# Summing eight products: GpSimd's halving and two VectorE adds replaced by one VectorE tensor_reduce

## What is computed

```
x = x + layernorm(attention(layernorm(x)))
x = x + layernorm(ffn(layernorm(x)))

# attention: 512-wide rows are cut in tokens of C = 16 channels, two branches of 8 channels;
# a window has 8 tokens (a row piece in one branch, a column piece in the other)
attn = softmax(q * 8**-0.5 @ k.T)          # 8 x 8 for each window
out  = attn @ v + depthwise_conv(v)
att  = concat(branch0, branch1) @ proj_w + proj_b
tok  = tok + layernorm(att) * ln_w + ln_b
```

## Time and profile before

| | us |
|---|---|
| runs of the kernel before (3) | 1411.92, 1413.1, 1414.27 |
| median | 1413.1 |
| span of the profiled execution | 1412.0 |
| VectorE busy in it | 1243.1 |
| TensorE busy in it | 1044.9 |
| GpSimd busy in it | 765.3 |
| ScalarE busy in it | 523.5 |

### The profile page before, as it was taken

The page is one execution under the profiler, slowest core; times in us unless marked ns, Lnnn a source line. Parts: engine busy times, 40 slices in busy tenths (PEclk is TensorE's granted clock), DMA queues, the critical chain, the costliest instruction groups (busy, mean ns, idle before and its releaser), DMA issues. The chain is left out here.

```text
span 1412.0 us, 14344 instructions
## 1 busy us (share of the span) xinstructions
PE 1044.9 (74%) x4483; PEld 531.0 (38%) x4483; DVE 1243.1 (88%) x1716; ACT 523.5 (37%) x790; POOL 765.3 (54%) x492
## 2 busy tenths in 40 slices
PE   5524368777887688868787778876887688678896
PEld 3312244343443343434343334433444244233442
DVE  4999999999899999999899998999899999975313
ACT  2235335332452434414253324524344143523332
POOL 2555336565576555765456644765557664754322
PEclk9756669889898899979898899988899799889998
DMA  4100200103001210102101030012101020012000
GB/s 128 30 0 13 77 6 24 30 1 89 1 16 45 60 31 1 38 21 59 30 3 57 0 89 1 15 45 59 30 1 46 15 60 1 7 53 60 7 24 30
DMA packets 70266, 46.07 MB, mean 33 GB/s; under 512 B 39616, under 2 KB 64192, under 8 KB 70208
## 3 DMA queue, kind: packets, MB, share of 16 engines
q1 hardware_dynamic: 65344, 45.10, 11.5%
q10 hardware_dynamic: 4864, 0.32, 0.2%
HBM read 28.63 MB, written 16.78 MB: 32 GB/s over the span
## 5 line engine op out<-in xcount | busy, mean ns | idle before, releaser
L599 PE MATMUL ps_up<-xhi,wu 128*128 128x512 f16 x512 | 218.8, 427 | 145.1 <-DVE fuse L1190 144.9
L864 POOL TENSOR_TENSOR sum<-prod 128x1024 f32<-128x1024 f32 x64 | 154.4, 2412 | 171.1 <-DVE prod L1031 171.1
L873 POOL TENSOR_TENSOR sum<-prod 128x1024 f32<-128x1024 f32 x64 | 158.6, 2478 | 156.4 <-DVE prod L1031 156.4
L1031 DVE TENSOR_TENSOR prod<-probs,qkvl 128x512 f32<-128x512 f32 x256 | 240.0, 1000 | 0.0
L1031 DVE TENSOR_TENSOR prod<-qkvl 128x512 f32<-128x512 f32 x256 | 222.2, 927 | 6.3 <-ACT qkvl L713 6.3
L599 PE MATMUL ps_up<-xlo,wu 128*128 128x512 f16 x512 | 218.2, 426 | 0.0
L599 PE MATMUL ps_gate<-xhi,wg 128*128 128x512 f16 x512 | 207.5, 405 | 3.6 <-DVE xlo L1183 3.2
L599 PE MATMUL ps_gate<-xlo,wg 128*128 128x512 f16 x512 | 205.5, 401 | 0.0
L926 POOL TENSOR_TENSOR flo<-fuse,fhi 128x512 f16<-128x512 f32 x128 | 172.8, 1351 | 59.2 <-ACT fhi L772 59.2
L766 ACT ACTIVATE gact<-ps_gate,sgate 128x512 f32<-128x512 f32 x128 | 87.7, 685 | 231.4 <-PE ps_gate L599 231.2
L1190 DVE SCALAR_TENSOR_TENSOR fuse<-ps_up,sup,gact 128x512 f32<-128x512 f32 x128 | 95.3, 744 | 77.0 <-PE ps_up L599 70.4
(11 more groups left out here) (169 smaller groups left out, 1719.2 us busy)
## 6 DMA issues: line engine op xcount, KB each, us to landing
xb<-in_L_attn_x SPq DMA_DIRECT2D x64, 128.0 KB, 2.6
xr<-in_L_attn_x SPq DMA_DIRECT2D x16, 512.0 KB
attn_rows<-ratt SPq DMA_DIRECT2D x16, 512.0 KB, 2.9
o<-attn_rows SPq DMA_DIRECT2D x32, 256.0 KB, 3.8
out_x<-o SPq DMA_DIRECT2D x14, 512.0 KB
x<-in_L_ffn_w_gate SPq DMA_DIRECT2D x1, 1024.0 KB, 5.4
xr<-in_L_ffn_w_up SPq DMA_DIRECT2D x1, 1024.0 KB, 7.6
out_x<-o SPq DMA_DIRECT2D x4, 256.0 KB
```

Of the source, the lines that this page charges most:

```text
L599: mm = nc.tensor.matmul(ps[:], w[:, k, :], xs[:, k, :], start=(k == 0 and part == 0), stop=(k == KB - 1 and part == 1))
L864: nc.gpsimd.tensor_tensor(dst.rearrange("p (s c) -> p s c", c=4), s[:, :, 0:4], s[:, :, 4:8], ALU.add).then_inc(half_done, 1)
L873: nc.gpsimd.tensor_tensor(dst.rearrange("p (w jc) -> p w jc", jc=4 * HB), s[:, :, 0:4 * HB], s[:, :, 4 * HB:], ALU.add).then_inc(half_done, 1)
L1031: a = nc.vector.tensor_tensor(dst, left(g, br, w), right(g, br, w), ALU.mult)
```

## The change

GpSimd no longer works on the sums: its `qk` and `pv` steps, the tile `sum4` and the semaphore `half_done` are gone. On VectorE `reduce_unit` now waits for `prod_done` and makes one `tensor_reduce` over 2048 elements with 256 outputs. For the scores the reduced axis is the channel, innermost in memory. For the values it is the key j, which has a step of 8 floats. `products` now waits, for a free `prod` buffer, on the reduction two units earlier instead of on GpSimd. The chain has 12 links instead of 20, and all waits on it are renumbered.

```diff
-ATT_LINKS = 20
+ATT_LINKS = 12
+SUM_LINKS = (1, 2, 4, 5, 8, 9, 10, 11)
...
-            def qk(at, u, ut, uq):
...
-                src, dst = halve(n, u, 0)
-                sum4_free(n, u, 0)
-                s = src.rearrange("p (s c) -> p s c", c=HB)
-                nc.gpsimd.tensor_tensor(dst.rearrange("p (s c) -> p s c", c=4), s[:, :, 0:4], s[:, :, 4:8],
-                                        ALU.add).then_inc(half_done, 1)
...
-            def pv(at, u, ut, uq):
...
-                s = src.rearrange("p (w jc) -> p w jc", jc=WIN * HB)
-                nc.gpsimd.tensor_tensor(dst.rearrange("p (w jc) -> p w jc", jc=4 * HB), s[:, :, 0:4 * HB],
-                                        s[:, :, 4 * HB:], ALU.add).then_inc(half_done, 1)
...
-                need(dve, half_done, 2 * UNITS * n + UNITS * stage + u - 1)
+                i = UNITS * stage + u - 2
+                need(dve, att_chain, ATT_LINKS * n + SUM_LINKS[i] if i >= 0 else ATT_LINKS * (n - 1) + SUM_LINKS[i])
...
-                dve.wait_ge(half_done, 2 * UNITS * n + UNITS * stage + u + 1)
-                link = ATT_LINKS * n + ([1, 3, 6, 8][u] if stage == 0 else 12 + 2 * u)
+                dve.wait_ge(prod_done, 2 * UNITS * n + UNITS * stage + u + 1)
                 if stage == 0:
-                    a = sum4[:, u % 2, :].rearrange("p (s c) -> p s c", c=4)
-                    lo, hi, one, two = a[:, :, 0:2], a[:, :, 2:4], a[:, :, 0], a[:, :, 1]
+                    a = prod[:, u % 2, :].rearrange("p (s c) -> p s c", c=HB)
                 else:
-                    a = sum4[:, u % 2, :].rearrange("p (w jc) -> p w jc", jc=4 * HB)
-                    lo, hi, one, two = a[:, :, 0:2 * HB], a[:, :, 2 * HB:], a[:, :, 0:HB], a[:, :, HB:2 * HB]
-                nc.vector.tensor_tensor(lo, lo, hi, ALU.add).then_inc(att_chain, 1)
-                dve.wait_ge(att_chain, link)
-                nc.vector.tensor_tensor(dst, one, two, ALU.add).then_inc(att_chain, 1)
+                    a = prod[:, u % 2, :].rearrange("p (w j c) -> p w c j", j=WIN, c=HB)
+                    dst = dst.rearrange("p (w c) -> p w c", c=HB)
+                nc.vector.tensor_reduce(dst, a, AX.X, ALU.add).then_inc(att_chain, 1)
```

More of the change, by code:

```diff
@@ L96, in sandwich_kernel @@
         prod = sb("prod", [P, 2, 4 * WIN * WIN * HB])
-        sum4 = sb("sum4", [P, 2, 1024])
         probs = sb("probs", [P, 2, WIN, WIN, WIN])
@@ L175, in sandwich_kernel @@
         prod_done = sem("prod_done")
-        half_done = sem("half_done")
         sub_done = sem("sub_done")
@@ L666, in warm_cat @@
             def warm_cat(at, ut, uq):
-                pe.wait_ge(att_chain, ATT_LINKS * (2 * at[0] + at[1]) + 18)
+                pe.wait_ge(att_chain, ATT_LINKS * (2 * at[0] + at[1]) + 10)
                 warm(0, 8, ut, uq)
@@ L845, in token_bias @@
                                         ALU.add).then_inc(xl_done, 2)
[L847 to L856, removed]
-            def qk(at, u, ut, uq):
-                t, g = at
-                n = 2 * t + g
-                src, dst = halve(n, u, 0)
-                sum4_free(n, u, 0)
-                s = src.rearrange("p (s c) -> p s c", c=HB)
-                nc.gpsimd.tensor_tensor(dst.rearrange("p (s c) -> p s c", c=4), s[:, :, 0:4], s[:, :, 4:8],
-                                        ALU.add).then_inc(half_done, 1)
-            def pv(at, u, ut, uq):
[L868 to L871, removed]
-                s = src.rearrange("p (w jc) -> p w jc", jc=WIN * HB)
-                nc.gpsimd.tensor_tensor(dst.rearrange("p (w jc) -> p w jc", jc=4 * HB), s[:, :, 0:4 * HB],
-                                        s[:, :, 4 * HB:], ALU.add).then_inc(half_done, 1)
             def attn_add(at, ut, uq):
@@ L879, in attn_add @@
                     return
-                pool.wait_ge(att_chain, ATT_LINKS * (2 * t + g) + 20)
+                pool.wait_ge(att_chain, ATT_LINKS * (2 * t + g) + 12)
                 add_attention(nc.gpsimd, g)
@@ L962, in cent_out_first @@
                 cent_out(at, ut, uq)
-            walk(pool, {"ln1_fin": ln1_fin, "token_bias": token_bias_first, "qk": qk, "pv": pv, "attn_out": attn_add,
+            walk(pool, {"ln1_fin": ln1_fin, "token_bias": token_bias_first, "attn_out": attn_add,
                         "cent_out": cent_out_first, "ffn_norm1": ffn_norm1,
@@ L1053, in attn_at @@
             def attn_at(u):
-                return attn[:, u // 2, 4 * (u % 2):4 * (u % 2) + 4].rearrange("p w i c -> p (w i) c")
+                return attn[:, u // 2, 4 * (u % 2):4 * (u % 2) + 4].rearrange("p w i c -> p (w i c)")
             def qk(at, u, ut, uq):
@@ L1075, in softmax @@
                 n = 2 * t + g
-                dve.wait_ge(att_chain, ATT_LINKS * n + 4 + 5 * br)
+                dve.wait_ge(att_chain, ATT_LINKS * n + 2 + 3 * br)
                 pr = probs[:, br].rearrange("p w i j -> p (w i) j")
                 nc.vector.tensor_reduce(smax[:, br, :], pr, AX.X, ALU.max).then_inc(att_chain, 1)
-                dve.wait_ge(att_chain, ATT_LINKS * n + 5 + 5 * br)
+                dve.wait_ge(att_chain, ATT_LINKS * n + 3 + 3 * br)
                 nc.vector.tensor_tensor(pr, pr, smax[:, br, :, None].broadcast_to([P, WIN * WIN, WIN]),
@@ L1097, in pv_norm @@
                                         ALU.add).then_inc(att_chain, 1)
-                dve.wait_ge(att_chain, ATT_LINKS * n + 11)
+                dve.wait_ge(att_chain, ATT_LINKS * n + 7)
                 nc.vector.reciprocal(ssum[:], ssum[:])
@@ L1108, in attn_out @@
                 n = 2 * t + g
-                dve.wait_ge(att_chain, ATT_LINKS * n + 19)
+                dve.wait_ge(att_chain, ATT_LINKS * n + 11)
                 o = attn[:].rearrange("p b w i c -> p (b w i) c")
@@ L1113, in attn_out @@
                 if on_vector(at):
-                    dve.wait_ge(att_chain, ATT_LINKS * n + 20)
+                    dve.wait_ge(att_chain, ATT_LINKS * n + 12)
                     add_attention(nc.vector, g)
```

## The result

| | us |
|---|---|
| before, median of 4 runs (1411.92 to 1414.27) | 1412.95 |
| changed, median of 4 runs (1446.3 to 1447.94) | 1447.28 |
| ratio, 95% interval | 1.0238, 1.0224 to 1.0253 |
| predicted | 1435.0 (1398 to 1478) |

The change makes the kernel 34 us slower. The profiled execution of the changed kernel took 1447.8 us, with a span of 1446.1 us, so about 1.7 us lie outside of the span.

A forecast was written before the change was run, and what follows sets the result against it. VectorE was taken to bound the kernel up to the last attention: 145 + 238 = 383 us added, 311 removed, 43 of stalls saved, 7 taken up by idle time, net +22 on 1412.0, so 1435 us (1398 to 1478).

The forecast's parts named there:

- The bound: VectorE sets the time from 30 to 1262 us (96% busy); the last 150 us go by TensorE.
- Score reductions: On VectorE, 64 added reductions reading in memory order, 2.27 us each, add 145 us.
- Value reductions: On VectorE, 64 added reductions at a 32-byte step, 0.71 ns an element dearer, 3.72 us each, add 238 us.
- Rival A: Faster: a strided read by a reduction on VectorE is free of the surcharge; about 1353 us; chance 12%.
- Rival C: Dearer: the strided value reduction costs up to 5.2 us, +93 us more, 1480 to 1528 us; chance 6%.
- Stalls: VectorE instructions that stay are held up less by GpSimd without halvings: 43 us saved, bounds 0 to 93.
- 0.88 to 0.93 forecast: Sign on VectorE's products: their mean should be 0.88 to 0.93 us instead of 0.96.
- Rival B: Not slower: with GpSimd's queue nearly empty, more than 72 us of VectorE stalls go; 1391 to 1412 us; chance 14%.
- every wait it adds is for VectorE's own earlier reduction: On VectorE: no case could be built of a wait left behind that keeps it idle; no time charged.
- Idle time: In VectorE's stretch, some 52 us of idle time take up 7 us of the added work.
- The last stretch: The last 150 us, from 1262 us to the end, should be as they are.

The follow-up runs named there:

- in-order run: Changed kernel with the 64 value-stage reductions reading prod in its order in memory, so summing channels instead of keys: 1354.9 us, ratio to before 0.958.
- v4: Kernel before with only the score sums done by one reduction a unit without GpSimd halving, value stage as before: 1366.2 us, ratio to before 0.9647.
- e2: Changed kernel with GpSimd's 128 halvings of prod put back, their results read by nobody: 1500.95 us, ratio to before 1.0608.

## Why the prediction was right, step by step

**The bound.** VectorE up to the last attention, TensorE after it: right. In all kernels timed here the span less VectorE's busy time stayed at 162 to 175 us while the span went from 1261 to 1500; ScalarE took 35 us of added work for at most 4 us more of waiting at VectorE (7.8 us against 3.9 in the in-order run), and the time stayed that of the in-order run.

**Score reductions.** 145 us expected, 144.2 measured.

**Value reductions.** 238 us expected, 243.2 measured. I priced them from an add with two strided inputs and from a strided write; the surcharge is 0.75 ns an element against the 0.71 taken. Rival A was wrong on the mechanism but right on the price: it said 1353 us, and the run without the strided read took 1354.9. What it had at 12% was that the surcharge would not come; it came. Rival C had it at up to 5.2 us a reduction; it stayed at 3.81.

**Stalls.** 43 us expected, 49 measured: 26.8 on products, 19.1 on L1080, 2.2 on L1173 and 1.1 on L1137. The sum was near. The products came out at a mean of 0.91 us, inside the 0.88 to 0.93 forecast. For L1080 the forecast had no place of its own, and it lost 19 of its 22 us. The score halvings had run beside it: with only them gone it is at 25.2 us (v4), with all halvings back at 44.8 (e2). Rival B did not come.

**The step that failed** inside a forecast that held is "every wait it adds is for VectorE's own earlier reduction", which I took for free. It isn't, where that reduction is the instruction just ahead: 58 times 124 ns, 80 of them a lost overlap and 44 idle, make 7.2 us. With it the books nearly close: 387.4 added, 306.8 removed, 49.2 of stalls, and 58 x 0.08 = 4.6 of lost overlap give +36.0 us of VectorE work; 35.8 were measured. To agree this closely is partly luck: small instructions that the sum leaves out became some 2 us shorter together.

**Idle time.** I let the 4 us of gaps between the adds go and 7 us more be taken up, 11 in all. Idle time fell by 3.7 us, or by 6.3 without the 2.6 us that the new wait added. The last stretch, which I had unchanged, became 2.5 us longer; that the lower granted clock makes it so is only argued, no run tried it.

So 22 us were forecast and 34 measured: +4 for the reductions, +7 for the wait, +5 for idle time, +2.5 for the end, -6 for stalls, within 1 us. The +7 is the price by the timeline; the run with three buffers gave back 3 to 5 of it. That the stalls missed toward the other side hid a third of the rest, and this is luck; the range held since it was 80 us wide.

## What to carry to other kernels

A reduction is a good replacement for a tree of adds only if it reads in order: 2.27 us for 2048 elements here, against 157 us / 64 = 2.5 us for three adds. At a step of 16 bytes or more it took 1.6 to 1.7 times as long. Before giving up, look for who writes the data: here a copy on an idle engine turned a loss of 2.4% into a gain of 4.3%.

Helper work on GpSimd is not free for a bound VectorE even when nobody waits for its result: halvings cost 52 us beside reductions, where nobody read them, and 151 us beside two-input adds. Ask which VectorE instructions will run beside it, and count inputs.

With two buffers, a wait for the engine's own last instruction is a wait too: 124 ns each time here.

## What the runs showed that I had not expected

A step of 64 bytes is cheaper than one of 32: 3556 against 3835 ns for 2048 elements, and 3774 at 16 bytes. The unit isn't the reason, since the same unit took 3812 ns at 32 bytes in the changed kernel. No run here tells why.

The 8-byte step, at 2228 ns, looks faster than reading in order, at 2274. It isn't: it stood at the first value unit, and in the in-order run the first value unit took 2228 ns as well (median of its 16), the other three 2276 to 2278. The line's minimum shows it, and so do its first two instances:

```profile
L1014 DVE TENSOR_REDUCE attn<-prod x64: 2227/2275/2289, 58.5 to 1192.8; 128x256 f32<-128x2048 f32 x64
...
58.54 2.23 DVE L1014 TENSOR_REDUCE attn<-prod 128x256 f32<-128x2048 f32 x1
...
63.29 2.28 DVE L1014 TENSOR_REDUCE attn<-prod 128x256 f32<-128x2048 f32 x1
```

Why it is some 48 ns shorter at that place stays open.

The price of the same GpSimd work differed by a factor of nearly three with what stood beside it on VectorE, and naming each stall after its neighbour found only 117 of the 151 us.
